# Router weights as the stationary operand, in four column quarters of TensorE, in an eight-core attention and expert-layer kernel

## The reference

```python
def _L0_ffn_ref(hidden_states, Wr, W1, b1, Wo, bo, gamma, beta):
    x = hidden_states.reshape(-1, H)
    router_logits = x @ Wr.T                       # Wr is 8 x 1024
    expert_idx = jnp.argmax(jax.nn.softmax(router_logits, axis=-1), axis=-1)
    for e in range(E):                             # E = 8, W1[e] is 1024 x 4096
        mask = (expert_idx == e)[:, None].astype(x.dtype)
        inter = inter + mask * jax.nn.gelu(x @ W1[e] + b1[e], approximate=False)
    y = inter @ Wo + bo + x
    ...                                            # layer norm with gamma and beta

xn = _layernorm(x, axis=-1)
x = x + _L0_attn_ref(xn, ...) + _L0_ffn_ref(xn, ...)
```

## Time and profile before

| | us |
|---|---|
| median of 3 runs | 1863.91 |
| their range | 1863.17 to 1867.79 |
| profiled execution | 1862.12 |
| its span (core 3, the slowest) | 1860.5 |
| spans of the eight cores | 1846.6 to 1860.5 |
| TensorE busy, share of the span | 91% |
| ScalarE, VectorE, GpSimd | 73%, 39%, 17% |
| first stage: router matmuls L843, busy, x256 | 39.3 |
| first stage: f32 transposes L829, busy, x128 | 24.1 |

### The profile page before, as it was taken

The page is one execution under the profiler, slowest core; times in us unless marked ns, Lnnn a source line. Parts: engine busy times, 40 slices in busy tenths (PEclk is TensorE's granted clock), DMA queues, the critical chain, the costliest instruction groups (busy, mean ns, idle before and its releaser), DMA issues.

```text
span 1860.5 us, 43159 instructions; the slowest of 8 cores (1846.6 to 1860.5 us)
## 1 busy us (share of the span) xinstructions
PE 1700.1 (91%) x15752; PEld 979.2 (53%) x15752; DVE 725.3 (39%) x1332; ACT 1351.5 (73%) x1540; POOL 322.3 (17%) x357
## 2 busy tenths in 40 slices
PE   5888998999989999999999997889799999999995
PEld 4774454454554454554554553334466666666652
DVE  5662354354354353353452453318303223323133
ACT  4767998999999999999999999995533332233210
POOL 2110000001000000000000000001232434533335
PEclk9889999999999999999999999999899999999998
DMA  8883334335545445445444446644876666665712
GB/s 229 236 208 67 69 70 75 69 70 86 103 76 102 70 70 86 69 79 88 69 71 69 69 70 156 153 101 160 279 251 200 228 203 214 215 216 195 234 68 98
DMA packets 54063, 243.95 MB, mean 131 GB/s; under 512 B 8160, under 2 KB 8672, under 8 KB 51552
## 3 DMA queue, kind: packets, MB, share of 16 engines
q0 software_dynamic: 25056, 137.91, 35.7%
q1 hardware_dynamic: 28368, 102.84, 17.3%
q10 hardware_dynamic: 432, 0.35, 0.1%
HBM read 295.59 MB, written 105.91 MB: 216 GB/s over the span
## 4 chain that ended last, share of the span: by engine, by line
PE 84%; issue 5%; DVE 5%; ACT 2%; DMA 2%; POOL 0%; DVEq 0%; ACTq 0%; POOLq 0%
PE acc L893 24%; PE sc L882 14%; PE zp L692 14%; PE yp L705 11%; PE fb L794 8%; PE fb L799 5%; PE yp L971 3%; PE fb L809 1%; DVE stA L1377 1%; DVE stB L1378 1%; PE fb L759 1%; PE lgp L843 1%; PE tp L829 1%; ACT xnf L1078 1%; DMA small<-small_c 1%
## 5 line engine op out<-in xcount | busy, mean ns | idle before, releaser
L1112 ACT ACTIVATE P<-sc,negm 128x1024 bf16<-128x1024 f32 x1024 | 1061.0, 1125 | 37.5 <-PE sc L882 32.4
L893 PE MATMUL acc<-P,V 64*128 64x512 bf16 x4096 | 627.6, 377 | 30.5 <-DVE stB L1378 28.8
L882 PE MATMUL sc<-QT,KT 64*128 64x512 bf16 x2048 | 405.4, 379 | 49.9 <-issue 29.8
L692 PE MATMUL zp<-xeT,w1r 128*128 128x288 bf16 x2048 | 291.3, 288 | 11.8 <-ACT hT L1018 11.8
L1018 ACT ACTIVATE hT<-zp,small 128x288 bf16<-128x288 f32 (+2 forms) x256 | 119.9, 469 | 243.2 <-PE zp L692 240.1
L893 PEld LDWEIGHTS acc<-P,V 64*128 64x128 bf16 x4096 | 224.6, 94 | 132.4 <-issue 55.9
L705 PE MATMUL yp<-wo,hT 128*128 128x512 bf16 x1088 | 271.5, 379 | 0.2 <-issue 0.2
L882 PEld LDWEIGHTS sc<-QT,KT 64*128 64x128 bf16 x2048 | 123.3, 93 | 269.1 <-issue 238.5
L692 PEld LDWEIGHTS zp<-xeT,w1r 128*128 128x128 bf16 x2048 | 201.3, 98 | 106.4 <-issue 12.8
L617 POOL DMA_DIRECT2D w1bf<-w_c x128 | 62.9, 492 | 899.8 <-ACT P L1112 899.8
L794 PE MATMUL fb<-xnT,wqkv 64*128 64x512 bf16 x1344 | 215.9, 379 | 2.8 <-DVE KT L1234 0.2
(11 more groups left out here) (146 smaller groups left out, 1259.1 us busy)
## 6 DMA issues: line engine op xcount, KB each, us to landing
w1bf<-w_c POOLq DMA_DIRECT2D x128, 512.0 KB, 5.6
w1r<-w1bf SPq DMA_DIRECT2D x128, 512.0 KB, 4.4
xt<-xseq SPq DMA_DIRECT2D x32, 512.0 KB, 6.1
xb_scr<-xnf POOLq DMA_DIRECT2D x16, 512.0 KB, 7.9
wo2bf<-wo_c POOLq DMA_DIRECT2D x16, 512.0 KB, 5.6
wo<-wo2bf SPq DMA_DIRECT2D x16, 512.0 KB, 5.0
res_scr<-rt SPq DMA_DIRECT2D x16, 512.0 KB, 3.2
xn_scr<-xnf POOLq DMA_DIRECT2D x16, 256.0 KB, 7.1
```

The costliest lines, as they stand in the source:

```text
L692: ins = te.matmul(zp[z % 2][:, 0:CAP], w1r[k % 8][:, kc * 256 + (ic % 2) * 128:kc * 256 + (ic % 2 + 1) * 128], xeT[:, kc * XR + lo:kc * XR ...
L882: ins = te.matmul(sc[n % 2][:, h * 512:(h + 1) * 512], KT[g % 2][h * 64:(h + 1) * 64, c * 128:(c + 1) * 128], QT[g % 2][h * 64:(h + 1) * 6 ...
L893: return te.matmul(acc[h][:, :], V[(n // 128) % 2][lo:lo + 64, c * 192 + h * 64:c * 192 + h * 64 + 128], P[n % 6][lo:lo + 64, h * 512:(h + ...
L1112: se.activation(out=P[n % 6][:, :], in_=sc[n % 2][:, :], func=AF.Exp, bias=negm[g % 2][:, :], scale=0.125).then_inc(s_P, 1)
```

## The change

The roles of the operands are exchanged. Wr's 128 x 8 piece, padded with zeros to 128 x 32, becomes the stationary operand, and the 128 x 128 transposed rows stream. The eight matmuls of a block go to four quarters of 32 columns of the array in turn (q = kc % 4), and so to four groups of 32 partitions of lgp, two matmuls being added up in each. This gives logits x tokens, four partial sums of them. VectorE copies that 128 x 128 tile to lsb, and a second matmul with lsb as the stationary operand and a 0/1 matrix `four` of 128 x 8 adds the four parts and turns the result to tokens x 8, at columns 256 + 8t of lgp. It runs in the iteration two after, ahead of the next block's router.

```diff
-        for dst, src in [(constf, cf_c), (constb, cb_c), (small, sm_h)]:
+        for dst, src in [(constf, cf_c), (constb, cb_c), (small, sm_h), (wrt, wr_h)]:
             se.dma_start(out=dst[:, :], in_=src[:, :]).then_inc(s_cst, 16)
...
+    for e in range(8):
+        cf[e::32, 145 + e] = 1.0
...
+        four = constf[:, 145:153]
+        lsb = [stA[:, j * 128:(j + 1) * 128] for j in range(2)]
+        wrt = stB[:, 0:256]
...  # TensorE
-            te.wait_ge(s_cst, 16 * 3)
+            te.wait_ge(s_cst, 16 * 4)
...
                 r = i - 3
+                if 2 <= r <= 32 and r % 2 == 0:
+                    t = r // 2 - 1
+                    te.wait_ge(s_rc, t + 1)
+                    te.matmul(lgp[:, 256 + t * 8:256 + (t + 1) * 8], lsb[t % 2], four,
+                              start=True, stop=True).then_inc(s_rt, 1)
                 if 0 <= r < 32 and r % 2 == 0:
                     t = r // 2
                     te.wait_ge(s_xf, t + 1)
                     for kc in range(8):
-                        ins = te.matmul(lgp[:, t * 8:(t + 1) * 8],
+                        q = kc % 4
+                        ins = te.matmul(lgp[32 * q:32 * q + 32, 0:128],
+                                        wrt[:, kc * 32:(kc + 1) * 32],
                                         xtf[t % 2][:, kc * 128:(kc + 1) * 128],
-                                        wrt[:, kc * 8:(kc + 1) * 8], start=(kc == 0), stop=(kc == 7))
-                    ins.then_inc(s_rt, 1)
+                                        start=(kc < 4), stop=(kc >= 4))
+                    ins.then_inc(s_rp, 1)
...  # VectorE
-            ve.wait_ge(s_cst, 16 * 3)
+            ve.wait_ge(s_cst, 16 * 4)
...
                     if t >= 2:
-                        ve.wait_ge(s_rt, t - 1)
+                        ve.wait_ge(s_rp, t - 1)
                         ve.wait_ge(s_xo, t - 1)
                     ve.tensor_copy(out=xtf[t % 2][:, :], in_=tp1[t % 2][:, :]).then_inc(s_xf, 1)
+                a = i - 4
+                if 0 <= a < 32 and a % 2 == 0:
+                    t = a // 2
+                    ve.wait_ge(s_rp, t + 1)
+                    if t >= 2:
+                        ve.wait_ge(s_rt, t - 1)
+                    ve.tensor_copy(out=lsb[t % 2],
+                                   in_=lgp[:, 0:128]).then_inc(s_rc, 1)
...
             ve.wait_ge(s_rt, 16)
-            ve.tensor_copy(out=lg[:, :], in_=lgp[:, 0:128]).then_inc(s_lg, 1)
+            ve.tensor_copy(out=lg[:, :], in_=lgp[:, 256:384]).then_inc(s_lg, 1)
...  # host: small_c without Wr (128 x 280), Wr by itself (128 x 256)
+    wrt_c = np.zeros((128, 8, 32), dtype=np.float32)
+    wrt_c[:, :, 0:8] = Wr.T.reshape(8, 128, 8).transpose(1, 0, 2)
```

More of the change, by code:

```diff
@@ L120, in build @@
     wo_h = nc.dram_tensor("wo_c", [128, 8 * 1024], F32, kind="ExternalInput").ap()
-    sm_h = nc.dram_tensor("small_c", [128, 344], F32, kind="ExternalInput").ap()
+    sm_h = nc.dram_tensor("small_c", [128, 280], F32, kind="ExternalInput").ap()
+    wr_h = nc.dram_tensor("wr_c", [128, 256], F32, kind="ExternalInput").ap()
     w1_h = nc.dram_tensor("w1_c", [NE * 16, 128, 2048], F32, kind="ExternalInput").ap()
@@ L134, in build @@
     wo2bf = nc.dram_tensor("wo2bf", [16, 128, 2048], BF16, kind="Internal").ap()
-    cf = np.zeros((128, 145), dtype=np.float32)
+    cf = np.zeros((128, 153), dtype=np.float32)
     cf[:, 0:128] = np.eye(128)
@@ L156, in sb @@
             return stack.enter_context(nc.sbuf_tensor(name, [128, cols], dt))
-        constf = sb(ctx, "constf", 145, F32)
+        constf = sb(ctx, "constf", 153, F32)
         constb = sb(ctx, "constb", 384, BF16)
-        small = sb(ctx, "small", 344, F32)
+        small = sb(ctx, "small", 280, F32)
         idf, w8, ecol = constf[:, 0:128], constf[:, 128:136], constf[:, 136:144]
@@ L164, in build @@
         idb, bones, up = constb[:, 0:128], constb[:, 128:256], constb[:, 256:384]
-        wrt, b1s = small[:, 0:64], small[:, 64:320]
-        bqs, bks, bvs = small[:, 320:328], small[:, 328:336], small[:, 336:344]
+        four = constf[:, 145:153]
+        b1s = small[:, 0:256]
+        bqs, bks, bvs = small[:, 256:264], small[:, 264:272], small[:, 272:280]
         epsA = sb(ctx, "epsA", 1, F32)
@@ L324, in build @@
         s_xp = sem("s_xp")
+        s_rp = sem("s_rp")
+        s_rc = sem("s_rc")
         s_rt = sem("s_rt")
@@ L1535 @@
         Wo.reshape(8, 128, 1024).transpose(1, 0, 2).reshape(128, 8192))
-    wrt_c = np.ascontiguousarray(
-        Wr.T.reshape(8, 128, 8).transpose(1, 0, 2).reshape(128, 64))
+    wrt_c = np.zeros((128, 8, 32), dtype=np.float32)
+    wrt_c[:, :, 0:8] = Wr.T.reshape(8, 128, 8).transpose(1, 0, 2)
+    wrt_c = np.ascontiguousarray(wrt_c.reshape(128, 256))
     w1_c = np.ascontiguousarray(
@@ L1545 @@
     small_c = np.ascontiguousarray(np.concatenate(
-        [wrt_c, b1_t, per_partition(L0_attn_bq), per_partition(L0_attn_bk),
+        [b1_t, per_partition(L0_attn_bq), per_partition(L0_attn_bk),
          per_partition(L0_attn_bv)], axis=1))
     shared = dict(wq_c=qkv_lay(Wq), wk_c=qkv_lay(Wk), wv_c=qkv_lay(Wv), wo_c=wo_c,
-                  w1_c=w1_c, wo2_c=wo2_c, small_c=small_c,
+                  w1_c=w1_c, wo2_c=wo2_c, small_c=small_c, wr_c=wrt_c,
                   bo_b=rows(L0_attn_bo), bo2_b=rows(L0_ffn_bo), ga_b=rows(L0_ffn_gamma),
```

## The result

| | before | changed |
|---|---|---|
| median, first comparison (6 runs each) | 1865.13 us | 1855.78 us |
| ratio of the undisturbed runs | | 0.995, 95% interval 0.9936 to 0.9964 |
| the changed kernel again, on another chip | 1862.15 us | 1854.96 us |
| ratio there | | 0.9964, 0.9951 to 0.9978 |
| profiled execution, its slowest core | 1862.12, 1860.5 us | 1858.14, 1856.6 us |

The change is 0.5% faster, 7 to 9 us. Some runs fell into a disturbed state of the chip, far above the rest; ratios leave them out, plain medians do not, and the profiled execution of the changed kernel is the slowest of the five that are left.

The account below looks back on a forecast made before the run. Core 3's chain of waits through the first stage was taken as the bound. Start +3.0, router -4.3, copies +1.2, clock -6.0 make -6.1: 1862.1 to 1856.0, with 1.8 for the median 1858 us; 8 in 10 range 1848 to 1870.

Parts of the forecast that it names:

- Where it acts: First stage, ending near 155 us: time won or lost there moves the span equally; first scores some 6 us earlier.
- the sign that the prediction set: If the first-stage end moves by another amount than the span, the reading that the rest only shifts is wrong.
- The start, +3.0: First instructions wait for a fourth constant transfer, wr_c: +3.0 us, between 0.5 by bytes alone and 3.6 at small's rate.
- The router group, 0.96 us: Router matmuls in quarters overlap by halves, nine steps of 0.107 us; with the sum, -4.3 us on the chain.
- The drain: Skill rule against the forecast: changing tiling mode drains TensorE, some 0.16 us each, making the sum 2.6 us worse.
- The sum, 0.21: Matmul adding the four quarters, ahead of the next router group: 0.21 us at the high clock, never waiting for VectorE.
- the copies, 0.28 x16: VectorE's sixteen PSUM copies of 128x128, 0.28 us each, mostly covered by other waits: +1.2 us on the chain.
- The clock, -6.0: More streamed columns keep TensorE's clock high in the first stage: -6.0 us, half of 12.4.
- What is late next: Transfers named as the next late neighbour, their share 1.03 from 31 to 54 us; no separate term.
- The first (no overlap): Rival: quarters don't overlap and the clock stays as it is; about +9.7 us, 1873.5 us, chance 0.17.
- The second: Rival: overlap as forecast, but the clock gains nothing or transfers eat its gain; -0.1 us, 1864 us, chance 0.32.
- The third: Rival: full overlap of quarters and a high clock through most of the stage; -14.5 us, 1849 us, chance 0.15.

Follow-up runs that it names:

- const4: Changed kernel's constants, four transfers and waits, but the router of the kernel before, without sum or copies: 1868.4 us, 1.002 of before.
- wide: Kernel before with each router matmul streaming Wr's eight columns sixteen times over (128 columns, a broadcast): 1857.2 us, 0.9965 of before.
- fill_late: Changed kernel plus four 384-column matmuls in TensorE's pause ahead of each own block's transposes from the third on: 1856.2 us, 0.9965 of before.
- fill: early plus four 384-column bf16 matmuls on TensorE ahead of each own block's transposes from the third on: 1848.5 us, 0.9927 of before.
- early: Changed kernel, VectorE waiting for no constant, TensorE for wr_c and small only before its first router group: 1843.7 us, 0.9887 of before.
- serial: Changed kernel with all eight router matmuls in quarter 0, so no overlap: 1864.5 us, 0.9996 of before.
- two: Changed kernel with the eight router matmuls in two quarters instead of four: 1856.3 us, 0.996 of before.

## Why the prediction was right

1858 us was forecast, with 1856.0 + 1.8 behind it, and 1855.8 was measured; 0.5% faster, inside the range. That the sum came near the truth is in part luck. The start cost 0.7 us more than forecast, the rest gained 2.2 us more, and that rest had been added up from two effects that don't add; each had been cut by guess.

- **Where it acts.** Right. The mean of first scores moved by 5.9 us and the latest core's by 5.4 (forecast 6.1); between the two cores with the longest span it is 9.2 (152.1 against 142.9), of which the later part gave 5.3 back. That the rest only shifts holds roughly: from first scores to the end it is 1703.7 us before and 1707.0 after in the means of the first profiles, 1705.6 in the second of the changed kernel. By the sign that the prediction set, the reading is off by these 2 to 3 us. Over all thirteen profiles this rest is 1703.7 to 1707.3 us, in no order of the kernels. Part of the 3 us is TensorE's clock at the stage's end: four of eight cores had a low stretch 5 to 6 us after their last scores (one before), and the output projection's matmuls were busy 57.6 us there instead of 55.9. Why it falls there in one execution and not in another was not tried.
- **The start, +3.0.** Measured +3.9 at bn_stats and +3.7 in time (const4). The upper bound of 3.6 was the better value, but not for its reason: small, 32 KB shorter, landed no earlier (14.0 us against 13.6, means of the cores), and wr_c's 128 KB came 3.5 us behind it.
- **The router group, 0.96 us.** Wrong in size: nine half-overlapped steps were assumed, four full ones are there, 0.46 us with the longer first one, and 0.1 behind them, 0.58 in all. The assumption was an order (first record, second record, next quarter) that the starts above refute: four starts come together, four times, so one record of each quarter goes before the second of any. (The rows don't name the record.) The row on row halves had spoken for overlap of separate quarters, and the argument from it stopped halfway. The step itself was right, 0.109 against 0.107.
- **The drain.** The Trainium skill's rule ("TensorEngine Tiling (Array Packing)", Key Properties: a change of mode drains the engine) fits the rows, with a price under what I gave it: the last step starts at 56.742 and needs 0.109, the next unit starts at 56.95, so 0.10 us behind the group; in front of it 56.185 + 0.107 against 56.370, 0.08. In the kernel before, where the mode stays, the next unit starts one step of 0.112 us behind the last router record. I had said 0.16 each. The Trainium skill's rule for three column tiles ("TensorE: Matmul & The Clock Gate", Part 3) gave the side that came; it says starts about 4 ns apart, here they are 7.
- **The sum, 0.21, and the copies, 0.28 x16.** As forecast: 0.22 from 56.15 to 56.37, and 281 ns. The copies are on the chain more often than I said, in nine of sixteen rounds of the slowest core (2.4 us against 1.2), where VectorE is now one of the engines that set the pace.
- **The clock, -6.0.** The step that failed as a cause of its own. Low-clock time did fall, by 9 us by the records (16 with the stretch before the first rise), and wide shows that with the old group length a high clock is worth 9 us of the stage. But taking more of it out of the changed kernel moved nothing (fill_late after 50 us, fill on the early form). Length and clock are two ways to the same 9 to 11 us: serial to two, 9.6 us with the same time at the low clock; before to wide, 9.1 us with nearly the same length. I had added them as independent terms, 4.3 and 6.0; the whole, 10.3 less 1.2 for the copies, met a real 11.3 (const4's first scores 154.6 against 143.3).
- **What is late next.** The forecast named the transfers and gave them no price. Behind the router stands no single engine: the chain of the changed kernel changes between ScalarE, VectorE, TensorE's transposes and projections, and the transfers of x blocks, 7 to 26 us of them in each core. The stage is 124 to 126 us in the changed kernel, two, fill_late and wide. What it would be with x blocks that come earlier, by more buffers for instance, no run tried.
- **The rivals.** The first (no overlap) can be read off serial, 0.9996 instead of the 9.7 us slower that was forecast for it, since there the clock did rise; its mechanism, VectorE waiting for the group, is real at 9.2 us. The second said 1864, 8 us too much, with the cause that is nearest to fill_late's result, a clock that gains nothing more; it took the router group at 4.3 us. The time that it also gave to no overlap with a rising clock, 1864, is what serial took, 1864.5, though by other terms: the clock brought 2.4 us of stage there, not 8. The third had the overlap right, and the gain wrong by the same missing limit: 1849 without asking what is late next.

## What to carry to other kernels

When two effects shorten work on the same engine, don't add them: take the distance to the next engine on the chain as the ceiling of both together, and look for it in the rounds where the chain already leaves the engine (three rounds of the earlier trace rows had shown it). A small weight matrix as the stationary operand in column quarters costs a quarter of the steps, but the copy that it adds on another engine must find the group done when its turn comes: in serial it didn't, and the gain was gone. A first wait on "all constants" deserves the question which of them the waiting engine uses: here the answer was none, and it was worth 11.6 us on the changed kernel, more than the change itself, and 6.1 us on the kernel before.

## What the runs showed of the hardware

- An f32 matmul is two records. With a full load of 128 columns their starts are 0.112 us apart at the high clock, with eight streamed columns as with 128: streaming sixteen times as much is nearly free behind the load (a group of sixteen takes 1.71 and 1.79 us up to the next unit's start).
- Column quarters of f32 matmuls run four abreast, starts 7 ns apart, 0.109 us a step at the high clock and 0.21 at the low.
- In core 3 of the kernel before, TensorE was busy 18.4 of the 19 us from 31 to 50 us with transposes and router, at the low clock, which rose at 54.2 us. Over the cores it rose at 39.5 to 54.4 us there, and in wide, the same work with 128 streamed columns, at 22.6 to 31.6 us.
- On ScalarE's queue, beside two busy queues, small's 172 KB landed 5.2 us behind constb before, and wr_c's 128 KB 3.5 us behind small after (means of the cores): 33 and 37 KB per us. In all, a fourth constant of 128 KB, 100 KB more on the queue, moved the first bn_stats by 3.9 us.
